# Lanes without a token gather a row of their own, and layer 1's row gathers wait for the landing three groups back

## The chip, the cores and the metric

The kernel runs on one core of a Trainium2 chip. The metric is the device time of one execution in microseconds (us), the median of several runs. Engines are named as the profile names them: PE (TensorE matmul), PEld (its weight load), DVE (VectorE), ACT (ScalarE), POOL (GpSimd) and SP (SyncE, which only issues DMAs here).

## The reference, cut to what matters

Two transformer layers over 4 x 1024 tokens of 128 features. Each layer ends in a feed-forward block with experts, in which one expert is chosen for each token. Layer 0 has 8 experts, layer 1 has 16 and a shared expert beside them:

```python
# layer 0: xt is (4096, 128)
probs = softmax(xt @ Wr + br);  gate, idx = max(probs), argmax(probs)
y = relu(xt @ W1[idx] + b1[idx]) @ W2[idx] + b2[idx]       # for each token its own expert
x = x + gb * y * gate
# layer 1
score = sigmoid(max(hidden @ router_w.T));  e = argmax
gate, up = split((hidden * score) @ gate_up_proj[e])
routed = (up * silu(gate)) @ down_proj[e]
shared = (silu(hidden @ shared_gate_w.T) * (hidden @ shared_up_w.T)) @ shared_down_w.T
x = x + gb * (shared + routed)
```

## The kernel before

**Tiles of one expert each.** The tokens of each expert are put into tiles of 128 lanes, and every expert starts a new tile. The number of tiles that this takes depends on the data, so the program always runs the most that can occur: `NS0 = NT + E0 = 40` in layer 0 and `NS1 = NT + E1 = 48` in layer 1 (`NT = 32` is 4096 tokens by 128). 48 tiles have 6144 lanes for 4096 tokens, so 2048 lanes of layer 1 hold no token (1024 in layer 0). Counting the experts that the router chooses for the reference's own inputs, the tokens of layer 1 fill or begin 39 tiles; tiles 39 to 47 hold no token at all. In layer 0 they take 37, and tiles 37 to 39 are empty.

**How the rows get into the tiles.** The normalised tokens lie in `M.h` (32 tiles of 128 x 128 f32) and are stored to HBM as `hrows0`, a row of 512 B for each token (SP, lines 255 to 258 in layer 0 and 1955 to 1961 in layer 1). The class `Dispatch` works out `gidx[lane, tile]`, the number of the row that a lane reads. In `sources` (lines 865 to 872) `psI[:, NS:2*NS]` is the token's tile plus 1, or 0 in a lane without token, and `psI[:, 0:NS]` is its lane. 128 x (tile plus 1) - 128, cut off at 0, plus the lane is the row. For a lane without token it gives 0: all of these lanes read row 0, the first token's. POOL then issues one indirect DMA (a gather of 128 rows, 64 KB) for each tile, line 984 in layer 0 and line 1997 in layer 1. The results of empty lanes are never read.

**The order around the change.** Each engine runs its own list in order, and engines wait for each other by semaphores. Tiles go in groups of `GT = 4`. In layer 1, POOL issues the 48 gathers; each adds to the semaphore `got` of its group (a ring of 4). Ahead of tile 8 POOL waits until groups 0 and 1 have landed, and ahead of each group q from 3 on until PE has turned group q - 2 (`x_T`). PE waits for `got` ahead of each group, turns the four tiles (line 2242), and then runs for each tile the two matmuls of line 2252, a transpose (line 2259) and the matmuls of line 2269. Gathers of tiles 0 to 31 land in `M.h`, those of tiles 32 to 47 in `spare`, a part of the buffer `shared_kept`, that the shared expert used before. Its last reader there is DVE (`gate`, which counts in `m_ready`).

**After the experts.** DVE copies each result to `y` (line 2149), SP stores it to `result1` (line 1965), and when all is stored POOL gathers the results back in token order (line 2007, 32 gathers). DVE multiplies and adds them (lines 2157 and 2164), between its steps for the last five parts of the shared expert (lines 1850, 1851, 1878, 1892 and 1903), and SP stores `out`.

Of the kernel before, what the change touches and what calls it, by code (L numbers as in the profile page):

```python
# [171 lines left out]
def phase_front(nc, D, M):  # L172

    at = turn_order()
    with Names(nc, "fr_") as n:
# [59 lines left out]
        with nc.Block() as block:  # L235
            @block.sync
            def _(sp):
                def load_x(b):
                    sp.dma_start(M.x[:, tiles_of(b), :], D["x"][b].rearrange("(t p) e -> p t e", p=P)).then_inc(ld_x[b], 16)

                sp.dma_start(cT[:], D["cT"]).then_inc(ld_c, 16)
                sp.dma_start(wmod0[:], D["wmod"][:, 0, :]).then_inc(ld_c, 16)
                load_x(0)
                for dst, src in qkv:
                    sp.dma_start(dst[:], src).then_inc(ld_qkv, 16)
                load_x(1)
                for dst, src in outer:
                    sp.dma_start(dst[:], src).then_inc(ld_o, 16)
                load_x(2)
                load_x(3)  # L250
                for dst, src in later[:EARLY_LOADS]:
                    sp.dma_start(dst[:], src).then_inc(ld_o, 16)
                for dst, src in later[EARLY_LOADS:]:
                    sp.dma_start(dst[:], src).then_inc(ld_later, 16)
                for b in range(B):
                    sp.wait_ge(h_ready, b + 1)
                    sp.dma_start(M.hrows0[b * L:(b + 1) * L, :].rearrange("(t p) e -> p t e", p=P),
                                 M.h[:, tiles_of(b), :]).then_inc(M.h_stored, 16)
                sp.wait_ge(ld_later, 16 * (len(later) - EARLY_LOADS))

# [480 lines left out]
class Dispatch:  # L741
# [123 lines left out]
    def sources(self, dve, link):  # L865

        NS = self.NS
        dve.wait_ge(self.inv_mm, 1)
        link(dve.tensor_scalar(self.tile_row[:], self.psI[:, NS:2 * NS], float(P), -float(P), ALU.mult, ALU.add))
        link(dve.scalar_tensor_tensor(out=self.tile_row[:], in0=self.tile_row[:], scalar=0.0, in1=self.psI[:, 0:NS],  # L870
                                      op0=ALU.max, op1=ALU.add))
        dve.tensor_copy(self.M.gidx[:, 0:NS], self.tile_row[:]).then_inc(self.idx_ready, 1)  # L872

    def ranks(self, pe):

# [32 lines left out]
def phase_ffn0(nc, D, M):  # L908

    E, NS = E0, NS0  # L910
    with Names(nc, "f0_") as n:
# [28 lines left out]
        with nc.Block() as block:  # L940
# [28 lines left out]
            @block.gpsimd  # L969
            def _(pool):  # L970
                link = Link(pool, pool_step)
                pool.wait_ge(M.h_stored, 16 * B)
                pool.wait_ge(disp.idx_ready, 1)

                for k in range(NS):
                    q = k // GT
                    if k % GT == 0:
                        if q >= 2 and q % 2 == 0:
                            pool.wait_ge(got[q - 1], 16 * GT)
                        if q == WINDOW:  # L980
                            pool.wait_ge(x0_T, GT)
                        elif q > WINDOW:
                            pool.wait_ge(x_T, q - WINDOW)
                    pool.indirect_dma_start(  # L984
                        out=row_tile(k), out_offset=None, in_=M.hrows0[:, :],
                        in_offset=bass.IndirectOffsetOnAxis(ap=M.gidx[:, k:k + 1], axis=0)).then_inc(first[k] if q == 0 else got[q], 16)
                bounded_gate_on(pool, link, M, tmp, 0, GB)
                pool.wait_ge(mod_out, B)
                cb = M.mod[:, 1, :, CB * P:(CB + 1) * P]
                link(pool.tensor_scalar(cb, cb, 1.0, None, ALU.add))  # L990
                bounded_gate_on(pool, link, M, tmp, 1, GA)
                bounded_gate_on(pool, link, M, tmp, 1, GB)
                for s in first:
                    pool.wait_ge(s, 16)
                for s in got[1:]:
                    pool.wait_ge(s, 16 * GT)
# [912 lines left out]
def phase_ffn1(nc, D, M):  # L1909

    E, NS, NC = E1, NS1, 2 * B
    with Names(nc, "f1_") as n:
# [3 lines left out]
        h_ready, h_T, hT_ready, lg_mm = n.sem("h_ready"), n.sem("h_T"), n.sem("hT_ready"), n.sem("lg_mm")  # L1916
        shifted, exp_done, gate_ready, rows_ready = n.sem("shifted"), n.sem("exp_done"), n.sem("gate_ready"), n.sem("rows_ready")
        ld_shared, ld_experts, h_stored = n.sem("ld_shared"), n.sem("ld_experts"), n.sem("h_stored")
        got = [n.sem(f"got{i}") for i in range(WINDOW + 1)]
        x_T, xT_ready, mm1_done, silu_done, g_ready = (n.sem("x_T"), n.sem("xT_ready"), n.sem("mm1_done"),  # L1920
                                                       n.sem("e_silu_done"), n.sem("g_ready"))
        g_T, gT_ready, mm2_done, y_ready = n.sem("g_T"), n.sem("gT_ready"), n.sem("mm2_done"), n.sem("y_ready")
# [25 lines left out]
        with nc.Block() as block:  # L1948
            @block.sync
            def _(sp):  # L1950
                for dst, name in ((M.wsg1, "wsg1"), (M.wsd1, "wsd1")):
                    sp.dma_start(dst[:], D[name]).then_inc(ld_shared, 16)
                for dst, name in ((M.wgu1, "wgu1"), (M.wdn1, "wdn1")):
                    sp.dma_start(dst[:], D[name]).then_inc(ld_experts, 16)
                for b in (B - 1, *range(B - 1)):
                    if b == B - 1:
                        sp.wait_ge(last_rows, 1)
                    else:
                        sp.wait_ge(rows_ready, b + 1)
                    sp.dma_start(hrows[b * L:(b + 1) * L, :].rearrange("(t p) e -> p t e", p=P),  # L1960
                                 M.h[:, b * TB:(b + 1) * TB, :]).then_inc(h_stored, 16)
                rows_out = M.result1.rearrange("(s p) e -> p s e", p=P)
                for q in range(NS // GT):
                    sp.wait_ge(y_ready, (q + 1) * GT)
                    sp.dma_start(rows_out[:, q * GT:(q + 1) * GT, :], y[q % 2]).then_inc(stored[q % 2], 16)
                for c in range(NC):
                    sp.wait_ge(x_steps, c + 1)
                    sp.wait_ge(shared.x_added, c + 1)
                    sp.dma_start(D["out"][c // 2].rearrange("(t p) e -> p t e", p=P)[:, 4 * (c % 2):4 * (c % 2) + 4, :],
                                 M.x[:, 4 * c:4 * c + 4, :]).then_inc(out_stored, 16)  # L1970
                sp.wait_ge(out_stored, 16 * NC)

            @block.gpsimd
            def _(pool):
# [14 lines left out]
                pool.wait_ge(disp.idx_ready, 1)  # L1989
                for k in range(NS):  # L1990
                    q = k // GT
                    if k == 2 * GT:
                        for done in range(2):
                            pool.wait_ge(got[done], 16 * GT)
                    if k % GT == 0 and q >= WINDOW:
                        pool.wait_ge(x_T, q - WINDOW + 1)
                    pool.indirect_dma_start(  # L1997
                        out=row_tile(k), out_offset=None, in_=hrows[:, :],
                        in_offset=bass.IndirectOffsetOnAxis(ap=M.gidx[:, k:k + 1], axis=0)).then_inc(got[q % len(got)], 16)
# [313 lines left out]
def declare(nc, M):  # L2313
# [9 lines left out]
    M.gate, M.zeros = M.sb("gate", [P, NT]), M.sb("zeros", [P, P])  # L2323
    M.slot, M.expert = M.sb("slot", [P, NT], I32), M.sb("expert", [1, NS1], I32)
    M.result1 = nc.dram_tensor("result1", [NS1 * P, P], F32).ap()
    M.hrows0 = nc.dram_tensor("hrows0", [NT * P, P], F32).ap()
    M.result0 = nc.dram_tensor("result0", [NS0 * P, P], F32).ap()
    M.gidx = M.sb("gidx", [P, NS1], I32)
    M.lane, M.pcol, M.ip1 = M.sb("lane", [P, P]), M.sb("pcol", [P, 1]), M.sb("ip1", [P, NT])
# [95 lines left out]
```

## Time and profile before

| | us |
|---|---|
| median of 3 runs | 1177.31 |
| lowest and highest run | 1174.46 and 1179.62 |
| the profiled execution | 1174.11 |
| its span in the trace | 1172.1 |
| outside the span (1174.11 - 1172.1) | 2.0 |

The profiled execution lies 3.2 us under the median of the three runs. Times in the rows are us from the span's start. In the span the layers' stages follow one another: layer 0's attention until about 130, layer 0's experts from 130 to 223, layer 1's attention until about 985, and layer 1's feed-forward block from there to the end.

### The profile page before, as it was taken

To read this page: it belongs to the slowest core of one execution; us is meant where nothing else is said; L and a number is where in the kernel's file an instruction comes from. 1 tells how busy PE (TensorE), PEld (TensorE's weight loads), DVE (VectorE), ACT (ScalarE), POOL (GpSimd) and SP (SyncE) were. 2 spreads that over 40 slices of the span, in tenths; PEclk is the share of its full clock that TensorE was granted. 3 is DMA by queue.
4 is the path that set the end of the run, shared out by engine and by line. 5 is a ranking of instruction groups with operands and counts; after the bars stand their busy time and mean duration, and the time that the engine had idled before them with its cause. 6 is when DMAs were issued, how large, how long until landed. Compare 5 with 4: busy or idle time off the path is not lost. (4 is left out here: it accounts for less than half of the span.)

```text
span 1172.1 us, 23749 instructions
## 1 busy us (share of the span) xinstructions
PE 1045.9 (89%) x9028; PEld 496.0 (42%) x9028; DVE 946.6 (81%) x1442; ACT 780.5 (67%) x1559; POOL 332.0 (28%) x467
## 2 busy tenths in 40 slices
PE   6897699587679999999999999999999989889797
PEld 4786599443311222222222222222222249467555
DVE  7975555478799999999999999999999719956345
ACT  4543334144414999999999999999999976524221
POOL 4732367667520000000000000000000026257264
PEclk9988899898976999999999999999999999999899
DMA  7011377319980012220122201222020002314623
GB/s 239 1 37 37 86 202 203 106 34 215 215 200 2 22 16 34 35 34 15 23 34 36 34 5 33 35 35 34 4 34 3 3 2 81 111 53 116 66 61 84
DMA packets 93975, 76.75 MB, mean 65 GB/s; under 512 B 42884, under 2 KB 72836, under 8 KB 93352
## 3 DMA queue, kind: packets, MB, share of 16 engines
q1 hardware_dynamic: 89000, 65.27, 23.6%
q0 software_dynamic: 4864, 9.97, 4.9%
q8 instruction: 73, 1.20, 0.5%
q14 instruction: 38, 0.31, 0.1%
HBM read 47.74 MB, written 27.39 MB: 64 GB/s over the span
## 5 line engine op out<-in xcount | busy, mean ns | idle before, releaser
L1462 DVE TENSOR_REDUCE mx<-p_psA 128x1 f32<-128x1024 f32 x512 | 585.1, 1214 | 9.4 <-PE p_psA L1625 9.4
L1553 ACT ACTIVATE p_pt<-p_psS 128x512 f32<-128x512 f32 x1024 | 548.2, 596 | 37.8 <-PE p_psS L1647 18.1
L1660 PE MATMUL p_acc<-p_pt,V 128*32 128x256 f32 x4096 | 328.4, 392 | 15.4 <-ACT attn L1544 13.8
L1625 PE MATMUL p_psA<-K,Q 48*128 48x512 bf16 x1024 | 319.8, 395 | 9.4 <-DVE mx L1462 7.8
L1647 PE MATMUL p_psS<-Q,K 51*128 51x512 bf16 x1024 | 310.0, 384 | 0.0
L1660 PEld LDWEIGHTS p_acc<-p_pt,V 128*32 128x32 f32 x4096 | 81.9, 108 | 211.1 <-ACT p_pt L1553 110.5
L1379 POOL TENSOR_TENSOR mr<-zeros,mx 128x16 f32<-128x16 f32 x32 | 7.1, 223 | 546.8 <-DVE mx L1462 546.8
L1625 PEld LDWEIGHTS p_psA<-K,Q 48*128 48x128 bf16 x1024 | 57.0, 95 | 232.8 <-DVE mx L1462 197.8
L1647 PEld LDWEIGHTS p_psS<-Q,K 51*128 51x128 bf16 x1024 | 62.6, 93 | 18.1 <-ACT p_pt L1553 12.6
L1067 DVE TENSOR_TENSOR f_h<-f_bank,b 128x512 f32<-128x512 f32 x40 | 27.7, 692 | 38.3 <-PE f_bank L1135 38.3
L1027 ACT ACTIVATE f_h1T<-f_h 128x512 f32<-128x512 f32 x40 | 25.1, 629 | 31.2 <-DVE f_h L1067 31.2
L2061 ACT ACTIVATE f_sg<-f_bank 128x128 f32<-128x128 f32 x48 | 13.3, 278 | 48.2 <-PE f_bank L2252 48.2
L1135 PE MATMUL f_bank<-f_xT,f_w 128*128 128x128 f32 x320 | 43.6, 281 | 0.0
L1144 PE MATMUL f_mod_ps<-w,f_h1T 128*128 x320 | 42.7, 279 | 0.0
L2007 POOL DMA_INDIRECT h<-result,slot x32 | 31.0, 968 | 36.7 <-DMA result<-f_shared_kept 18.9
L984 POOL DMA_INDIRECT h<-hrows,gidx x32 | 30.6, 955 | 38.2 <-DVE gidx L872 20.9
L1135 PEld LDWEIGHTS f_bank<-f_xT,f_w 128*128 128x128 f32 x320 | 40.3, 197 | 0.1
L1997 POOL DMA_INDIRECT h<-hrows,gidx x32 | 31.6, 988 | 29.6 <-DVE gidx L872 18.0
L1144 PEld LDWEIGHTS f_mod_ps<-w,f_h1T 128*128 128x128 f32 x320 | 39.6, 195 | 0.0
L1334 POOL DMA_INDIRECT h<-result,slot x32 | 33.2, 1036 | 18.7 <-issue 7.8
L1850 PE MATMUL f_bank<-hT_l,wsg 128*128 128x512 f32 x64 | 34.5, 621 | 3.6 <-ACT f_shared_kept L1861 1.9
L1865 ACT ACTIVATE f_shared_sg<-f_bank 128x512 f32<-128x512 f32 x20 | 11.9, 597 | 36.6 <-PE f_bank L1850 36.6
(336 smaller groups left out, 1442.1 us busy)
## 6 DMA issues: line engine op xcount, KB each, us to landing
f_w<-in_w SPq DMA_DIRECT2D x40, 256.0 KB, 3.6
Q<-q_rows SPq DMA_DIRECT2D x32, 192.0 KB, 4.6
K<-k_rows SPq DMA_DIRECT2D x32, 192.0 KB, 5.2
hrows<-h SPq DMA_DIRECT2D x8, 512.0 KB, 3.2
result<-f_shared_kept SPq DMA_DIRECT2D x12, 256.0 KB, 3.0
result<-f_y SPq DMA_DIRECT2D x10, 256.0 KB, 4.1
V<-v_rows SPq DMA_DIRECT2D x16, 144.0 KB, 5.8
x<-in_x SPq DMA_DIRECT2D x4, 512.0 KB, 5.5
```

The costliest lines, as they stand in the source:

```text
L984: pool.indirect_dma_start(out=row_tile(k), out_offset=None, in_=M.hrows0[:, :], in_offset=bass.IndirectOffsetOnAxis(ap=M.gidx[:, k:k + 1], ...
L1135: mm = pe.matmul(ps1[j % 2][:, c * P:(c + 1) * P], w1[j % RING][:, c * P:(c + 1) * P], xT[j // GT % 2][:, j % GT, :], start=True, stop=True)
L1144: mm = pe.matmul(psY[j % 2][:, 0:P], h1T[j % RING][:, c, :], M.w20[:, bass.ds(expert[j], 1), c, :], start=(c == 0), stop=(c == FC0 - 1))
L1334: pool.indirect_dma_start(out=M.h[:, i, :], out_offset=None, in_=M.result0[:, :], in_offset=bass.IndirectOffsetOnAxis(ap=M.slot[:, i:i + 1 ...
L1462: dve.tensor_reduce(mx[v % 2][:, h, qt:qt + 1], psA[t][:], AX.X, ALU.max).then_inc(a_max, 1)
L1553: act.activation(pt[s % 2][:, head_at(s, j), :], psS[k % 3][:], ACT.Exp, scale=INV_SCALE).then_inc(s_out, 1)
L1625: mm = pe.matmul(psA[t][:, c * 512:(c + 1) * 512], Q[g % NBUF][rows, pair, q0:q0 + P], K[g % NBUF][rows, pair, c * 512:(c + 1) * 512], sta ...
L1647: pe.matmul(psS[k % 3][:], K[g % NBUF][rows, h // 2, kc * P:(kc + 1) * P], Q[g % NBUF][rows, h // 2, half * 512:(half + 1) * 512], start=T ...
L1660: mm = pe.matmul(acc[VW * h:VW * (h + 1), cols], V[g % NBUF][:, kc, h * (HD + 1):h * (HD + 1) + VW], pt[s % 2][:, h, cols], start=(kc == 0 ...
L1850: pe.matmul(self.bank_g(k)[:], M.wsg1[:, f * P:(f + 1) * P], tok, start=True, stop=True).then_inc(self.g_mm, 1)
L1997: pool.indirect_dma_start(out=row_tile(k), out_offset=None, in_=hrows[:, :], in_offset=bass.IndirectOffsetOnAxis(ap=M.gidx[:, k:k + 1], ax ...
L2007: pool.indirect_dma_start(out=M.h[:, i, :], out_offset=None, in_=M.result1[:, :], in_offset=bass.IndirectOffsetOnAxis(ap=M.slot[:, i:i + 1 ...
```

## The change

Four edits. (1) `hrows0` gets 128 rows more, in front of the token rows; SP fills them once, at the start, with the identity matrix `M.ident` (64 KB), and stores the tokens 128 rows further on, in both layers. (2) `sources` no longer takes off 128, and its last step is a maximum with `pcol` (a column that holds the lane's number) in place of a copy: a token's row number is now at least 128 and stays, and a lane p without token gets row p. (3) POOL's gathers of layer 1 have a semaphore for each group of four, and ahead of group q from 3 on POOL waits until group q - 3 has landed, not for PE; the wait ahead of tile 8 goes. (4) Since nothing then ties POOL to PE, it waits for `m_ready` ahead of tile 32, the first in `shared_kept`.

```diff
@@ SP, start of the program
+                sp.wait_ge(ld_qkv, 16 * len(qkv))
+                sp.dma_start(M.hrows0[0:P, :], M.ident[:]).then_inc(M.h_stored, 16)
                 for b in range(B):
                     sp.wait_ge(h_ready, b + 1)
-                    sp.dma_start(M.hrows0[b * L:(b + 1) * L, :].rearrange("(t p) e -> p t e", p=P),
+                    sp.dma_start(M.hrows0[P + b * L:P + (b + 1) * L, :].rearrange("(t p) e -> p t e", p=P),
                                  M.h[:, tiles_of(b), :]).then_inc(M.h_stored, 16)
@@ Dispatch.sources (DVE, both layers)
-        link(dve.tensor_scalar(self.tile_row[:], self.psI[:, NS:2 * NS], float(P), -float(P), ALU.mult, ALU.add))
+        link(dve.tensor_scalar(self.tile_row[:], self.psI[:, NS:2 * NS], float(P), None, ALU.mult))
         link(dve.scalar_tensor_tensor(out=self.tile_row[:], in0=self.tile_row[:], scalar=0.0, in1=self.psI[:, 0:NS],
                                       op0=ALU.max, op1=ALU.add))
-        dve.tensor_copy(self.M.gidx[:, 0:NS], self.tile_row[:]).then_inc(self.idx_ready, 1)
+        dve.tensor_scalar(self.M.gidx[:, 0:NS], self.tile_row[:], self.M.pcol[:, 0:1], None, ALU.max).then_inc(self.idx_ready, 1)
@@ layer 0, POOL
-                pool.wait_ge(M.h_stored, 16 * B)
+                pool.wait_ge(M.h_stored, 16 * (B + 1))
@@ layer 1
-        got = [n.sem(f"got{i}") for i in range(WINDOW + 1)]
+        got = [n.sem(f"got{i}") for i in range(NS // GT)]
@@ layer 1, SP
-                    sp.dma_start(hrows[b * L:(b + 1) * L, :].rearrange("(t p) e -> p t e", p=P),
+                    sp.dma_start(hrows[P + b * L:P + (b + 1) * L, :].rearrange("(t p) e -> p t e", p=P),
@@ layer 1, POOL
-                    if k == 2 * GT:
-                        for done in range(2):
-                            pool.wait_ge(got[done], 16 * GT)
+                    if k == NT:
+                        pool.wait_ge(shared.m_ready, EK)
                     if k % GT == 0 and q >= WINDOW:
-                        pool.wait_ge(x_T, q - WINDOW + 1)
+                        pool.wait_ge(got[q - WINDOW], 16 * GT)
@@ declare
-    M.hrows0 = nc.dram_tensor("hrows0", [NT * P, P], F32).ap()
+    M.hrows0 = nc.dram_tensor("hrows0", [P + NT * P, P], F32).ap()
```

What stands in a row on POOL in layer 1's gathers, before. A semaphore's number serves several phases and is named here after the first of them, so only the places of the waits tell something: the two names ahead of tile 8 are the landings of groups 0 and 1, the single name from tile 12 on is PE's `x_T`.

```order
L1997 DMA h<-hrows,gidx 128x128 [waits f1_idx_ready,fr_mod_ready]
L1997 DMA h<-hrows,gidx 128x128 x7
L1997 DMA h<-hrows,gidx 128x128 [waits fr_rstd_ready,fr_stats_ready]
L1997 DMA h<-hrows,gidx 128x128 x3
L1997 DMA h<-hrows,gidx 128x128 [waits fr_norm2_act]
L1997 DMA h<-hrows,gidx 128x128 x3
```

The same place of the changed kernel, and below "..." its first gather into `shared_kept`:

```order
L1998 DMA h<-hrows,gidx 128x128 [waits f1_idx_ready,fr_mod_ready]
L1998 DMA h<-hrows,gidx 128x128 x11
L1998 DMA h<-hrows,gidx 128x128 [waits fr_stats_ready]
L1998 DMA h<-hrows,gidx 128x128 x3
L1998 DMA h<-hrows,gidx 128x128 [waits fr_rstd_ready]
L1998 DMA h<-hrows,gidx 128x128 x3
...
L1998 DMA f_shared_kept<-hrows,gidx 128x128 [waits fr_act_step,f1_m_ready]
L1998 DMA f_shared_kept<-hrows,gidx 128x128 x3
```

The first twelve gathers now stand in a row without a wait; from tile 12 on a wait for a landing (another semaphore each time) stands where the wait for PE stood, and tile 32 has `m_ready` as well.

On SP, between the loads at the start of the program and the stores of the token rows, there was before:

```order
L254 DMA bo<-in_bo 128x128
L254 DMA wr<-in_wr 128x16
L257 DMA hrows<-h 128x8x128 [waits fr_h_ready] x4
L235 UNCONDITIONAL_BRANCH [waits fr_ld_later]
```

and now:

```order
L254 DMA bo<-in_bo 128x128
L254 DMA wr<-in_wr 128x16
L256 DMA hrows<-ident 128x128 [waits fr_ld_qkv]
L259 DMA hrows<-h 128x8x128 [waits fr_h_ready] x4
L235 UNCONDITIONAL_BRANCH [waits fr_ld_later]
```

One DMA more, behind all loads and ahead of the first store of rows.

## Rows read from the trace of the kernel before

**Rows 1.** The page: the span and the packets of the queue that POOL's gathers use.
```profile
span 1172.1 us, 23749 instructions
...
q0 software_dynamic: 4864, 9.97, 4.9%
```

**Rows 2.** The chain that ended last, in order of time: start, us, what.
```profile
1027.89 0.52 PE f_bank L895 x8
...
1072.55 0.64 PE f_bank L2242 x4
...
1092.28 9.75 DMA f_shared_kept<-hrows,gidx
1102.08 0.66 PE f_bank L2242 x4
...
1109.12 2.28 DMA result<-f_shared_kept
...
1112.14 0.94 POOL h L2007
...
1115.89 3.10 DMA h<-result,slot
1119.02 0.70 DVE f_shared_kept L2157
```

**Rows 3.** Timeline of PE, layer 1's experts: start, us, instruction [idle before <-releaser].
```profile
1047.61 0.60 PE L2242 MATMUL f_bank<-ident,h 128*128 128x128 f32 x4
...
1076.65 0.63 PE L2242 MATMUL f_bank<-ident,h 128*128 128x128 f32 x4
...
1080.74 0.63 PE L2242 MATMUL f_bank<-ident,f_shared_kept 128*128 128x128 f32 x4
...
1087.17 0.66 PE L2242 MATMUL f_bank<-ident,f_shared_kept 128*128 128x128 f32 x4 [2.35 <-DMA f_shared_kept<-hrows,gidx]
...
1095.30 1.11 PE L2242 MATMUL f_bank<-ident,f_shared_kept 128*128 128x128 f32 x4 [4.04 <-DMA f_shared_kept<-hrows,gidx]
```

**Rows 4.** Timeline of POOL, layer 1's gathers.
```profile
1042.68 1.43 POOL L1997 DMA_INDIRECT h<-hrows,gidx  x1 [2.24 <-DMA h<-hrows,gidx]
...
1048.48 0.95 POOL L1997 DMA_INDIRECT h<-hrows,gidx  x1 [0.60 <-PE f_bank L2242]
...
1077.24 0.95 POOL L1997 DMA_INDIRECT f_shared_kept<-hrows,gidx  x1 [0.30 <-issue]
...
1091.03 0.95 POOL L1997 DMA_INDIRECT f_shared_kept<-hrows,gidx  x1 [0.30 <-issue]
1092.28 0.94 POOL L1997 DMA_INDIRECT f_shared_kept<-hrows,gidx  x1 [0.30 <-issue]
```

**Rows 5.** DMA queues from 1060 to 1074: packets, MB, share of 16 engines.
```profile
q0 software_dynamic: 361, 0.75, 23.9%
q1 hardware_dynamic: 1584, 0.79, 19.5%
```

**Rows 6.** The same from 1085 to 1099.
```profile
q0 software_dynamic: 225, 0.46, 85.2%
q1 hardware_dynamic: 528, 0.26, 6.2%
```

**Rows 7.** Stretches: length, busy us of PE, PEld, DVE, ACT, POOL, PEclk, DMA share, GB/s.
```profile
1094.00:1100.00 6.00, 4.70 (x16) 3.89 (x17) 1.86 (x5) 0.98 (x4) 0.00 (x0) 0.50 0.85 54
...
1121.00:1160.00 39.00, 38.91 (x182) 24.47 (x183) 18.07 (x28) 8.36 (x14) 23.37 (x25) 1.00 0.25 68
```

**Rows 8.** Line 1997: its gathers' time from issue to landing.
```profile
DMA to landing us min/median/max: 2.5/2.9/3.6
```

**Rows 9.** Layer 0, timelines of POOL (L984) and PE (L1121).
```profile
130.42 1.22 POOL L984 DMA_INDIRECT h<-hrows,gidx  x1 [20.93 <-DVE gidx L872]
...
181.46 0.94 POOL L984 DMA_INDIRECT f_spare<-hrows,gidx  x1 [3.24 <-DMA h<-hrows,gidx]
...
190.21 0.95 POOL L984 DMA_INDIRECT f_spare<-hrows,gidx  x1 [0.30 <-issue]
...
142.97 1.12 PE L1121 MATMUL f_bank<-ident,h 128*128 128x128 f32 x4 [4.19 <-DMA h<-hrows,gidx]
...
206.12 0.60 PE L1121 MATMUL f_bank<-ident,f_spare 128*128 128x128 f32 x4
```

**Rows 10.** Timelines of SP at the start, and of DVE in layer 1's routing.
```profile
22.55 0.76 SPq L254 DMA_DIRECT2D wr<-in_wr  x1
65.64 44.23 SPq L257 DMA_DIRECT2D hrows<-h  x4
...
1028.44 0.21 DVE L869 TENSOR_SCALAR f_tile_row<-f_bank 128x48 f32<-128x48 f32 x1 [0.61 <-PE f_bank L895]
...
1028.92 0.19 DVE L872 CAST gidx<-f_tile_row 128x48 int32<-128x48 f32 x1
```

## The prediction, made before the changed kernel ran

> **What bounds the kernel now.** I read the chain that ended last first, because the change touches only two short stretches of a long kernel. In layer 1's experts the chain runs over PE up to 1072.55, then over POOL's issues to the last one at 1092.28, then through 9.75 us of a gather in flight, to PE's last group at 1102.08 [rows 2]. So the end of the expert stage is set by the landing of the last gather, and all behind it is tied to it: the store of the last results (1109.12), the gathers back (1112.14), and DVE's first use of them (1119.02), which stands ahead of DVE's steps for the shared expert [rows 2].
>
> Next, the timeline of PE. Groups 7 and 8 are turned at 1076.65 and 1080.74: 4.10 us for a group when nothing is missing [rows 3]. (Groups 2 to 8 all keep this step.) Group 9 then starts at 1087.17 after 2.35 us of idling, group 10 at 1095.30 after 4.04 us, both released by gathers [rows 3], group 11 at 1102.08 [rows 2]. With PE alone they would stand at 1084.84, 1088.94 and 1093.04.
>
> Why do these gathers land so late? POOL issues one each 1.25 us (1091.03 to 1092.28) [rows 4], and one normally lands 2.5 to 3.6 us after its issue, median 2.9 [rows 8]. The DMA queues show it. The program has 152 gathers (40 and 48 of rows in, 32 and 32 back) and 4864 packets on their queue [rows 1], 32 for each. From 1060 to 1074, 361 packets took 23.9% of 16 engines' 14 us [rows 5]: 53.5 us, 0.148 us each, so 32 of them keep the 16 engines for 0.30 us. From 1085 to 1099, 225 packets took 85.2% [rows 6]: 190.8 us, 0.85 us each, 1.70 us for a gather. That is more than the 1.25 us between two issues, so a backlog grows.
>
> What differs in these gathers? Not other traffic: the other queue took 19.5% in the quick stretch and 6.2% in the slow one [rows 5, 6]. Not the destination: group 8 goes to the same buffer, its last gather was issued at 1077.24 [rows 4] and PE started on it at 1080.74 without idling [rows 3], so it landed within 3.5 us. What differs is the content: tiles 39 to 47 hold no token, and each of their 128 lanes reads row 0. The late groups are just those with these tiles (9, 10 and 11). I conclude that 128 reads of one row of HBM are served nearly one after the other.
>
> **The change part by part.** The rows of empty lanes (edits 1 and 2). In the changed kernel a gather of an empty tile reads 128 different rows, 64 KB in a piece. No such gather is in the trace. Bounds: as quick as a gather of token rows, 0.30 us of the engines [rows 5], or no quicker than now, 1.70 us [rows 6]. I take the first, since there too all rows differ. The choice need not be exact: anything under POOL's 1.25 us leaves no backlog.
>
> POOL's waits (edit 3). Two stalls go: 2.24 us ahead of tile 8 and 0.60 us ahead of tile 12 [rows 4], each less the 0.30 us that stands ahead of every issue: 1.94 + 0.30 = 2.24 us. The new wait holds all later gathers and the gathers back behind it. It is for a gather issued 9 places back, 9 x 1.25 = 11.3 us, against a landing after 3.6 us at the most [rows 8]; even 9.75 us [rows 2] is under it. It costs nothing. The wait for `m_ready` ahead of tile 32 costs nothing either: PE's experts start, behind the shared parts that it counts, at 1047.61 [rows 3], some 24 us before tile 32 is issued. POOL's last issue moves from 1092.28 to 1090.04.
>
> Which is then the last? By POOL: 1090.04 and the time from a gather's issue to its reader. In the quiet stretch behind, that was 1119.02 - 1115.89 = 3.13 us [rows 2]. This gives group 11 at 1093.17. By PE: 1093.04. The two are almost level, and the later one gives 1102.08 - 1093.17 = **8.9 us saved**. With a landing of 3.6 us in place of 3.1 it would be 8.4, and never more than PE's 9.04 us. Groups 9 and 10 come out the same way: their last gathers are issued at about 1080.0 and 1085.0 and are there at 1083.2 and 1088.2, before PE wants them at 1084.84 and 1088.94. PE's clock, 0.50 from 1094 to 1100 [rows 7] behind its idling, counts for nothing in the sum, since PE waited for landings before and after that stretch.
>
> The Trainium skill (DMA: Bandwidth & Descriptors, the section on the anatomy of one DMA) gives the time of such a DMA as about 2.0 us plus bytes by 436 GB/s, whatever it reads; for 64 KB that is an estimate of 2.15 us, for the nine empty tiles as for any. This trace doesn't agree: 0.30 and 1.70 us of the engines for the same bytes. By the page, lane addresses would not matter and edits 1 and 2 would bring nothing; that is the first rival below.
>
> Does the gain reach the end? Between 1102.08 and 1119.02 each link waits for the one before [rows 2], and then PE is busy 38.91 of the 39 us from 1121 to 1160 [rows 7] with work that DVE's first use of the results released. Nothing there has a start of its own, so the whole moves forward.
>
> What it costs. DVE's last step of the routing: the copy took 0.19 us and a `TENSOR_SCALAR` of the same size 0.21 [rows 10]: 0.02 us, twice, and dropping the addition saves nothing that shows: 0.0. The identity rows: one more issue on SP (0.76 us for the one before it) into the idle time between 23.3 and 65.64 [rows 10]; its landing is asked for only ahead of the first gather at 130.42 [rows 9]. It costs nothing while that gap is there, and 0.8 us if it weren't. PE's first links of the stage (L895 at 1027.89 [rows 2]) don't change.
>
> Layer 0. It has the same cure for tiles 37 to 39, but no path to shorten. Their last gather is issued at 190.21 and PE turns that group at 206.12 [rows 9], 15.9 us later, with no idling between. POOL's stalls there (3.24 us ahead of tile 32, others alike) stay and are hidden too. PE's idle 4.19 us ahead of 142.97 [rows 9] is for group 1, in which the counts put only nine empty lanes: between 0 and 0.4 us, and I take 0.
>
> The sum: 1174.11 - 8.9 = 1165.2 us for the profiled execution. The median of the runs shown lies 3.2 us over that execution, so I forecast a median of 1177.31 - 8.9 = **1168.4 us**, 0.76% less. A measurement of this kernel can tell about 0.5%, 5.9 us, from no change.
>
> **The rivals.** (a) The row isn't the cause, and gathers of empty tiles stay at 1.70 us. Then only the 2.24 us of POOL's stalls remain, since the backlog begins that much earlier: 1175.1, no change that can be told. For it: no row of before has an empty tile that reads different rows. Against it: destination and traffic are excluded above, and only these nine tiles are slow. 10%.
>
> (b) The clock. It falls to half for stretches like the 6 us from 1094 on [rows 7]. If such a stretch comes into the shared part, in which PE bounds and now has 1.00 from 1121 to 1160 [rows 7], it costs up to 6.0 x 0.5 = 3.0 us: 1171.4. Against it: the fall at 1094 stood behind PE's idling of 2.35 and 4.04 us, and just this idling goes. 6%.
>
> (c) Slower: different rows are read worse than one row, for all nine tiles come back to the same 64 KB shortly after each other. The nine gathers begin to be read near 1083 and now end at 1102. (1102.1 - 1083.1) / 9 = 2.1 us for a gather is the point from which the kernel is slower; at 3.4 us, twice the present 1.70, the last lands near 1083.1 + 30.6 = 1113.7, 11.6 us late: 1188.9. For it speaks only that it isn't in the trace; against it the quick gathers of token rows. 4%.
>
> **How the numbers follow.** The forecast has 80%: 1168.4. Its own range goes from the lowest of the three runs less PE's 9.04 us, 1165.4, to the highest less 8.4, 1171.2. I take 1.1 us more below, since three runs may not show their lowest and layer 0 may give 0.4, and reach up to 1172.5, which takes in (b) with an unlucky median; (a) and (c), 14%, are left out. Faster by over 0.5%: the forecast and half of (b), 0.83. Within: (a) and the other half of (b), 0.13. Slower: 0.04.
>
> **What would show it.** In the trace of after: PE without idling ahead of groups 9 to 11, group 11 near 1093; POOL's last issue of a row gather near 1090; less than 35% of the engines for POOL's queue in the last 14 us of the gathers, and about 0.30 us a gather; no fall of the clock there; the back gathers starting near 1103; layer 0 as long as before. The cause is wrong if tiles 39 to 47 still take over 1.25 us each; the path is wrong if group 11 starts near 1093 and the end has not moved by 8 to 9 us.

## The result, and the profile after

| | before | after |
|---|---|---|
| median of 4 runs, us | 1176.26 | 1163.84 |
| lowest and highest | 1174.46 and 1179.62 | 1162.37 and 1166.31 |
| profiled execution | 1174.11 | 1166.31 |
| its span | 1172.1 | 1164.2 |

The ratio of the times is 0.9895, with a 95% interval from 0.9871 to 0.9918: 9.6 to 15.2 us saved, 12.4 between the medians. The forecast was 8.9 us saved and a range down to 1164.3, and the median lies 0.5 us below that range. The two profiled executions differ by 7.9 us. The difference between 7.9 and 12.4 is where these two executions lie among the runs: before 2.2 us under its median, after 2.5 us over it, as the slowest of four. That the kernel would later be slower than before on other chips could not be seen here; it is told below.

The traces show the forecast's path. PE's timeline in layer 1 (start, us, instruction), the last step of the routing and then groups 0, 8 and 11 of the kernel after:

```profile
1027.22 0.52 PE L897 MATMUL f_bank<-f_who,f_ohlo 128*128 128x96 bf16 x8 [0.78 <-DVE f_ohlo L855]
...
1048.64 0.60 PE L2243 MATMUL f_bank<-ident,h 128*128 128x128 f32 x4
...
1081.76 0.63 PE L2243 MATMUL f_bank<-ident,f_shared_kept 128*128 128x128 f32 x4
...
1094.06 0.63 PE L2243 MATMUL f_bank<-ident,f_shared_kept 128*128 128x128 f32 x4
```

The rows with idle times of [rows 3] are gone: from group 8 to 11 there are three steps of 4.10 us, 12.30 in all, where before they took 21.34 (1080.74 to 1102.08): 9.04 us less. POOL's timeline, the first and the last row gather and the first gather back:

```profile
1029.28 1.39 POOL L1998 DMA_INDIRECT h<-hrows,gidx  x1 [18.01 <-DVE gidx L874]
...
1089.22 0.94 POOL L1998 DMA_INDIRECT f_shared_kept<-hrows,gidx  x1 [0.30 <-issue]
1104.09 0.94 POOL L2008 DMA_INDIRECT h<-result,slot  x1 [13.92 <-DMA result<-f_shared_kept]
```

The last row gather is issued at 1089.22 (forecast 1090.04, with a stage that begins 0.6 us earlier), and the gathers back begin at 1104.09 in place of 1112.14 [rows 2]. The queues over the last 14 us of the row gathers, 1077 to 1091 (packets, MB, share of 16 engines), and line 1998's landings:

```profile
q0 software_dynamic: 362, 0.76, 21.0%
q1 hardware_dynamic: 1586, 0.79, 19.5%
```
```profile
DMA to landing us min/median/max: 2.4/2.5/3.5
```

21.0% of 16 x 14 us for 362 packets is 0.13 us a packet, 0.26 us of the engines for a gather, where the gathers of empty tiles had 1.70 [rows 6]. They are as cheap as gathers of tokens.

One thing had moved the other way. These are stretches of the kernel after (length, busy us of PE, PEld, DVE, ACT and POOL, PEclk, DMA share, GB/s), the first in the shared part ahead of the experts:

```profile
1028.00:1031.00 3.00, 3.00 (x5) 1.17 (x4) 2.95 (x7) 0.60 (x1) 1.41 (x2) 0.50 0.00 0
1094.00:1100.00 6.00, 5.69 (x36) 4.58 (x35) 3.92 (x14) 2.87 (x14) 0.00 (x0) 1.00 0.21 64
```

and this is the first of them in the kernel before:

```profile
1028.00:1031.00 3.00, 3.00 (x15) 1.56 (x15) 2.49 (x7) 1.19 (x2) 1.11 (x1) 1.00 0.00 0
```

The clock is 1.00 from 1094 to 1100, where it was 0.50 before [rows 7]. But it had fallen to half, 1.2 GHz, at 1028, in a part in which PE sets the pace. PE had idled three times in the routing just ahead of it, for 0.7 to 0.8 us each; before, it idled there in the same way, and the clock stayed at 1.00. So these two traces don't show why it fell. Group 0 is turned 21.4 us after PE's last step of the routing (line 897, 1027.22), where before it was 19.7 us (1027.89 to 1047.61). This execution lost 1.7 us there, and without it would have saved 9.6. In terms of the last group: 9.04 us gained by PE, 1.7 lost to the clock and 0.7 by which the routing ended earlier give 8.0, and group 11 stands 8.02 us earlier.

### The profile page after: what moved, and what is told of

The parts are those of the page before. It is cut to its first block and busy times, and to the rows that moved or that the text cites. A ratio compares the mean times of both kernels' runs of the same rounds, so it can differ in the third digit from the quotient of the medians.

```text
span 1164.2 us, 23750 instructions
## 1 busy us (share of the span) xinstructions
PE 1044.9 (90%) x9028; PEld 493.3 (42%) x9028; DVE 948.4 (81%) x1442; ACT 780.3 (67%) x1559; POOL 329.8 (28%) x467
## 5 line engine op out<-in xcount | busy, mean ns | idle before, releaser
L1029 ACT ACTIVATE f_h1T<-f_h 128x512 f32<-128x512 f32 x40 | 25.2, 629 | 31.5 <-DVE f_h L1069 31.5
L986 POOL DMA_INDIRECT h<-hrows,gidx x32 | 30.5, 953 | 38.0 <-DVE gidx L874 20.9
```

Of the source, the lines that this page charges most:

```text
L986: pool.indirect_dma_start(out=row_tile(k), out_offset=None, in_=M.hrows0[:, :], in_offset=bass.IndirectOffsetOnAxis(ap=M.gidx[:, k:k + 1], ...
```

## The experiments

I made 18 runs on five chips. The first eight fell on chips 14 and 8, the next four on chip 9, four on chip 6 and the last two on chip 10. It turned out that there are two kinds of chips here, so the kernel before stands beside each. The chip of the first measurement has no number on record.

### The parts alone, on chips 14 and 8

Own rows without the new waits, against the change (also rows_only_2 and rows_only_3):

```diff
-                    if k == NT:
-                        pool.wait_ge(shared.m_ready, EK)
+                    if k == 2 * GT:
+                        for done in range(2):
+                            pool.wait_ge(got[done], 16 * GT)
                     if k % GT == 0 and q >= WINDOW:
-                        pool.wait_ge(got[q - WINDOW], 16 * GT)
+                        pool.wait_ge(x_T, q - WINDOW + 1)
```

> Each empty lane reads a row of its own, in both layers, but the row gathers of layer 1 keep the waits of the kernel before (groups 0 and 1 landed ahead of tile 8, PE's transposes from tile 12 on). Row theory: tiles 39 to 47 land as quickly as any; the last issue stays near 1092.3, the last group starts at 1092.3 + 3.1 = 1095.4 in place of 1102.1, so 6.7 us are saved and PE waits about 1 to 2 us in all for rows. Rival (the row is not the cause): tiles 39 to 47 stay at 1.70 us of the engines each, and nothing is saved. If another 3 us of the measured gain (12.4 us between the medians, where the two profiled spans differ by 7.9) also belong to the rows, this kernel saves 9 to 10 us.

The new waits without own rows, against the kernel before (also waits_only_2 and waits_only_3):

```diff
-        got = [n.sem(f"got{i}") for i in range(WINDOW + 1)]
+        got = [n.sem(f"got{i}") for i in range(NS // GT)]
@@ layer 1, POOL
-                    if k == 2 * GT:
-                        for done in range(2):
-                            pool.wait_ge(got[done], 16 * GT)
+                    if k == NT:
+                        pool.wait_ge(shared.m_ready, EK)
                     if k % GT == 0 and q >= WINDOW:
-                        pool.wait_ge(x_T, q - WINDOW + 1)
+                        pool.wait_ge(got[q - WINDOW], 16 * GT)
```

> Empty lanes read row 0 as before; the row gathers of layer 1 wait for the landing three groups back. Row theory: the gathers of empty tiles still take 1.70 us each and only start 2.24 us earlier, so 2.2 us are saved and PE still waits some 5 to 7 us ahead of groups 9 to 11. Rival: the waits bring the greater part, 6 us or more. If the new wait can hold POOL, it shows here, where landings are latest: an idle time of POOL ahead of one of the last groups.

Own rows in layer 1 only, against the change:

```diff
-        dve.tensor_scalar(self.M.gidx[:, 0:NS], self.tile_row[:], self.M.pcol[:, 0:1], None, ALU.max).then_inc(self.idx_ready, 1)
+        if NS == NS1:
+            dve.tensor_scalar(self.M.gidx[:, 0:NS], self.tile_row[:], self.M.pcol[:, 0:1], None, ALU.max).then_inc(self.idx_ready, 1)
+        else:
+            dve.tensor_copy(self.M.gidx[:, 0:NS], self.tile_row[:]).then_inc(self.idx_ready, 1)
```

> The changed kernel, but in layer 0 the empty lanes read row 0 (all the same row, as before); layer 1 as changed. Theory that layer 0 hides its three empty tiles behind 15.9 us of slack: the time of the changed kernel within 0.5 us, about 1164. Rival, that the surplus of the measured gain over 8.9 us comes from layer 0: 3 us slower than the changed kernel, about 1167.

And the changed kernel itself:

> The changed kernel once more, beside the others on one chip. If the gain is the 9 us of PE's path, five rounds give 1167 beside 1176; if the measured gain of 12 us is real they give 1164. The trace shows which of the two profiled spans was the odd one: with no fall of the clock in the shared part ahead of the experts, group 0 starts about 1.0 to 1.7 us earlier than 1048.64 and the span is near 1162.

Measured on chip 14 (median us; ratio to the kernel before, 1203.06):

| kernel | us | ratio, 95% interval |
|---|---|---|
| rows_only | 1203.25 | 0.9995 (0.9971 to 1.0019) |
| waits_only | 1237.12 | 1.0283 (1.0246 to 1.0321) |
| rows_layer1 | 1239.61 | 1.0298 (1.0259 to 1.0337) |
| after_again | 1238.71 | 1.0306 (1.0268 to 1.0344) |

None of my numbers held except that layer 0's rows make no difference (rows_layer1 against after_again, within 1 us of each other). The kernel before was 27 us slower than on the first chip, and the changed kernel was slower than it by 36 us. The new waits alone made it so. (That layer 0's rows make no difference is thus measured on this chip alone.) I asked four again, with the kernel before for its trace:

> The kernel before, unchanged, for its trace. In the last four runs the kernel before took 1203 us and the changed kernel 1239, where the first measurement gave 1176 and 1164; there PE stood still for up to 2.4 us between two matmuls while POOL issued gathers. If that belongs to the chip, one of two pictures comes: 1176 and PE without such gaps ahead of 1080, or 1203 with gaps of 1 to 4 us in PE from tile 12 of the gathers on. In either, the last group is turned 9.0 us or more behind PE's own pace (tiles 39 to 47 read one row).

> The changed kernel once more. If the odd times belong to the chip of the last runs and this is another: 1164 to 1168, 9 to 12 us under the kernel before. If they come from the changed kernel itself (POOL issuing all 48 gathers without a pause), it is slower than the kernel before again, by 30 us or more, wherever it runs.

> Own rows for empty lanes, with the waits of before, once more. Where PE has no gaps: 6.7 us under the kernel before by my sum (the last gather issued near 1092.3, its group started at 1095.4), and 9 to 10 us if the surplus over the forecast belongs to the rows. Where PE has gaps: no difference, as in the last runs, since PE and not the last landing ends the stage.

> Row 0 for all empty lanes, with the new waits, once more. Where PE has no gaps: 2.2 us under the kernel before, PE waiting 5 to 7 us for the last three groups. Where PE has gaps: 30 us slower than before, since POOL then isn't paced by PE.

They came to chip 8 and repeated the picture beside the kernel before at 1203.88 (19 runs): before_again 1203.29, after_third 1236.15 (1.027, 1.0214 to 1.0325), rows_only_2 1204.18 (0.9995, 0.997 to 1.002) and waits_only_2 1236.2 (1.0244, 1.0203 to 1.0284).

Where does the time go? PE's timeline of after_again, in the shared part of layer 1 ahead of the experts (line 1894, 96 small matmuls; 10.7 us in the kernel before):

```profile
1052.28 6.86 PE L1894 MATMUL f_bank<-wsd,f_m 128*128 128x128 f32 x58
1060.69 0.60 PE L1894 MATMUL f_bank<-wsd,f_m 128*128 128x128 f32 x4 [1.54 <-issue]
...
1098.68 0.37 PE L1894 MATMUL f_bank<-wsd,f_m 128*128 128x128 f32 x1 [2.43 <-issue]
1101.48 0.37 PE L1894 MATMUL f_bank<-wsd,f_m 128*128 128x128 f32 x1 [2.43 <-issue]
...
1109.88 0.37 PE L1894 MATMUL f_bank<-wsd,f_m 128*128 128x128 f32 x1 [2.43 <-issue]
1111.28 0.37 PE L1894 MATMUL f_bank<-wsd,f_m 128*128 128x128 f32 x1 [1.03 <-issue]
...
1113.38 1.23 PE L1894 MATMUL f_bank<-wsd,f_m 128*128 128x128 f32 x5 [0.33 <-issue]
```

From 1082 on PE issues one matmul each 2.8 us and waits for nothing that the profile knows; ahead of that its gaps are shorter, mostly 1.0 to 1.8 us. POOL's timeline of the same run shows when this begins and ends:

```profile
1045.34 1.39 POOL L1998 DMA_INDIRECT h<-hrows,gidx  x1 [18.02 <-DVE gidx L874]
...
1059.94 0.95 POOL L1998 DMA_INDIRECT h<-hrows,gidx  x1 [0.30 <-issue]
...
1105.41 0.94 POOL L1998 DMA_INDIRECT f_shared_kept<-hrows,gidx  x1 [0.30 <-issue]
```

The first gap opens at 1059.14 (1052.28 + 6.86), between the issues of the eleventh and the twelfth gather in an unbroken row, and the last one of 2.43 us ends at 1109.88, 4.5 us behind the last issue. In the kernel before the waits break this row up: POOL stops ahead of tile 8 and then for PE. On chip 8 the kernel before has such gaps as well, but fewer and shorter ones. This is POOL in before_again, and below it PE's last group there:

```profile
1109.27 0.95 POOL L1997 DMA_INDIRECT f_shared_kept<-hrows,gidx  x1 [1.34 <-remote]
...
1115.35 0.94 POOL L1997 DMA_INDIRECT f_shared_kept<-hrows,gidx  x1 [1.39 <-remote]
...
1121.42 0.95 POOL L1997 DMA_INDIRECT f_shared_kept<-hrows,gidx  x1 [1.36 <-remote]
```
```profile
1136.12 0.63 PE L2242 MATMUL f_bank<-ident,f_shared_kept 128*128 128x128 f32 x4
```

A group takes 6.07 us there where PE alone needs 4.10. PE idles about 2 us in each group and POOL 1.3 us between two groups, for PE's turning of an earlier one: as I read it, they hold each other back. The last landing ends nothing (PE turns group 11 without idling), and own rows have nothing to shorten (rows_only 0.9995 twice). That the row cost itself is the same on these chips is told by the queue of waits_only on chip 14, from 1101 to 1110, and of after_again, from 1098 to 1107:

```profile
q0 software_dynamic: 166, 0.35, 88.8%
```
```profile
q0 software_dynamic: 224, 0.46, 19.1%
```

0.77 us a packet with row 0 for all, 0.12 with own rows.

### What keeps PE from issuing

Four kernels that change only the row gathers of layer 1. plain_pool and plain_sp replace them by plain loads, half_rows halves their bytes, paced spreads them by a multiplication on POOL ahead of each but the first (its operand is cleared once at the start):

```diff
@@ plain_pool (plain_sp: the same loop on SP)
-                    pool.indirect_dma_start(
-                        out=row_tile(k), out_offset=None, in_=hrows[:, :],
-                        in_offset=bass.IndirectOffsetOnAxis(ap=M.gidx[:, k:k + 1], axis=0)).then_inc(got[q % len(got)], 16)
+                    r = P + (k % NT) * P
+                    pool.dma_start(row_tile(k), hrows[r:r + P, :]).then_inc(got[q % len(got)], 16)
@@ half_rows
-                        out=row_tile(k), out_offset=None, in_=hrows[:, :],
+                        out=row_tile(k)[:, 0:P // 2], out_offset=None, in_=hrows.rearrange("r (a e) -> (r a) e", a=2),
@@ paced (filler, filler2: 128 x 256; declared and cleared above)
+                    if k > 0:
+                        link(pool.tensor_tensor(filler2[:], filler[:], filler[:], ALU.mult))
```

> POOL's 48 row gathers of layer 1 are replaced by plain DMAs that POOL issues: tile k loads 128 rows that follow one another, whichever tokens they are, so the routed results are not the reference's; waits, bytes and destinations as in the changed kernel. Question: what keeps PE from issuing (up to 2.4 us between two matmuls) on the chips where the changed kernel takes 1236 to 1239 us. Theory A, POOL's way of issuing (it writes the descriptors of each DMA): the gaps stay, about 1236. Theory B, the indirection itself: the gaps go, about 1180. If the kernel before takes 1176 here, there are no gaps to explain and the time is near 1160.

> The same plain loads, issued by SP with the same waits; POOL issues nothing until the gathers back. Again the routed results are not the reference's. Theory A (POOL's issuing disturbs PE): PE has no gaps in layer 1's experts, groups of 4.1 us, about 1180 where the changed kernel takes 1236. Theory C (the transfers themselves, 64 KB in 128 descriptors of 512 B, whoever issues them): gaps as in the changed kernel, 1236.

> The row gathers of layer 1 bring only the first 256 B of a row's place (a wrong half row for most lanes, so the routed results are not the reference's), with as many descriptors. If bytes are what matters, PE's gaps shrink by about half and 1236 becomes 1200 to 1210; if the number of gathers or descriptors matters, nothing changes: 1236.

> The changed kernel with a small multiplication on POOL (128 x 256, some 0.6 us) and its semaphore between two row gathers of layer 1, so that they come each 2 us and not each 1.25. If gathers issued too closely fill something that PE needs (the sum of issues and pauses in the runs so far fits with one gather each 2 us as what it can bear), PE's gaps go and its part of the shared expert ahead of the experts ends near 1064 in place of 1114; the last gather is then issued near 1045 + 47 x 2 = 1139 and the kernel takes about 1215 in place of 1236. If each gather costs PE a fixed time, however they are spaced, it stays at 1236 or is slower.

They came to chip 9, where the kernel before takes 1180.16 and PE has no gaps: 1166.73, 1169.58, 1168.89 and 1196.5 us, one execution each. On the gaps they say nothing. They do say what ends the stage. With plain loads all rows are there long before they are needed, and from the first load to PE's last group it is still 64.5 us (plain_pool, 1030.29 to 1094.82), as from the first gather in the changed kernel, 64.8 (1029.28 to 1094.06): PE alone bounds the stage by now. And paced shows the chain: PE waits for landings again, its last group starts at 1123.39 and not at 1094.06 (29.3 us later), and the span is 1194.7 and not 1164.2 (30.5 us longer).

The last two runs repeated two of them, and came to chip 10 (kernel before 1206.21, one execution):

> Plain loads of 128 consecutive rows in place of layer 1's row gathers, issued by POOL at 0.54 us each (the routed results are not the reference's). Only a chip of the kind of 14 and 8 (kernel before near 1203) tells something: about 1236 if any DMA that POOL issues keeps PE from issuing, about 1190 if it takes indirect gathers. On a chip of the other kind (kernel before near 1177): 1166, as twice.

> The changed kernel with a small POOL instruction between the row gathers of layer 1, so that they come each 1.9 us. On a chip of the kind of 14 and 8: if what counts is how closely gathers are issued, PE's gaps shrink or go, its shared part ends before 1075, and the kernel takes about 1215, less than the changed one (1236); if each gather costs PE a fixed time, 1236 or more. On a chip of the other kind: 1196, as once.

plain_pool_3 took 1188.84, paced_2 1215.81. Two rows of PE's timeline in plain_pool_3, the first of the experts and the next row with an idle time behind 1074 (46 us later), and then the list of PE's waits in paced_2 from 1040 to 1160 (us, times, longest), its first three:

```profile
1071.96 1.12 PE L2252 MATMUL f_bank<-wgu,f_shared_kept 128*128 x4 [1.76 <-DVE f_shared_kept L2137]
...
1120.17 0.48 PE L2269 MATMUL f_bank<-wdn,f_gT 128*128 x2 [0.17 <-ACT f_gT L2067]
```
```profile
PE f_bank L2247 <- DMA h<-hrows,gidx: 11.1, 5, 3.5
PE f_bank L2247 <- DMA f_shared_kept<-hrows,gidx: 10.0, 4, 3.7
PE f_bank L897 <- DVE f_ohlo L855: 2.3, 3, 0.8
```

Both expectations held on this chip, the first within 2 us. Without indirect gathers in layer 1 PE has no gap there, although POOL issues its DMAs faster (0.54 us each). With indirect gathers 1.9 us apart it has none either: no wait for "issue" is left in the list, where after_again had 42.4 us of them.

This tells something only if chip 10 has gaps at all, and neither of its runs is the changed kernel. Layer 0 settles it. Its 40 row gathers are indirect in every kernel of this document and 1.25 us apart, up to eight in a row. In plain_pool_3, POOL's first of them, and then PE:

```profile
130.58 1.21 POOL L986 DMA_INDIRECT h<-hrows,gidx  x1 [20.64 <-DVE gidx L874]
```
```profile
136.89 0.33 PE L1115 MATMUL f_bank<-ident,h 128*128 128x128 f32 x1 [0.85 <-issue]
...
164.81 1.15 PE L1146 MATMUL f_mod_ps<-w,f_h1T 128*128 x8 [1.59 <-issue]
...
220.78 0.60 PE L1123 MATMUL f_bank<-ident,f_spare 128*128 128x128 f32 x4
```

From the first gather to PE's last group layer 0 takes 90.2 us here, and 75.7 in the kernel before [rows 9]. The same stretch sorts all traces: 86.7 to 91.0 us in the ten from chips 14, 8 and 10, whatever the kernel, and 74.6 to 76.6 in the other ten. So one execution on chip 10 has gaps where gathers are 1.25 us apart and none where plain loads are 0.54 us apart, and another (paced_2) none where gathers are 1.9 us apart. On these three chips it is indirect gathers issued close together that keep PE from issuing. In layer 0 they do so within the first eight gathers, so the number after which it begins is not fixed. It also explains the kernel before on these chips: in before_again layer 0's stretch is 12.7 us longer than in the first trace of before (88.4 against 75.7) and layer 1's, from the first gather to group 11, 12.5 us (84.7 against 72.2). That is 25.2 us, where the medians on chips 8 and 6 lie 26 us apart. (The execution before_again is itself a long one of its kernel, and its span exceeds the first by 35.7 us; the rest lies elsewhere.)

The paced kernel on chip 10 is 20 to 23 us faster than the changed one on chips 14 and 8 (a comparison across chips), but still slower than the kernel before by 10 us, since 48 gathers then take 91 us. What gathers and PE share is not settled. In after_again no fetch of instructions is recorded from 1056 to 1112, where the changed kernel had six packets of them on the first chip: more fetching is not the cause, but a fetch that is held back is not excluded.

### The parts alone, where PE has no gaps

> The changed kernel. Where the kernel before takes 1176 to 1180: 9 to 12 us less, PE without idling ahead of its last groups; 9 if the surplus of the first measurement was chance, 12 if it is real. Where the kernel before takes 1203: 33 to 36 us more, as twice now.

> Own rows, waits of before. Without gaps in PE: 6.7 us saved (last gather issued near 1092.3, last group at 1095.4), so about 2.2 us behind the changed kernel. With gaps: as the kernel before, as twice now.

> Row 0 for all empty lanes, new waits. Without gaps in PE: 2.2 us saved, PE still waiting 5 to 7 us for its last groups; the queue of POOL's gathers takes over 80% of the 16 engines in the last 14 us. With gaps: 33 us slower than before.

> Plain loads of 128 consecutive rows in place of layer 1's row gathers, issued by POOL (the routed results are not the reference's). On chip 9 it took 1166.7, PE without gaps. On a chip with gaps: about 1236 if any DMA that POOL issues makes them, about 1190 if only indirect gathers do.

All four ran on chip 6, with the kernel before at 1177.3 (19 runs):

| kernel | us | ratio, 95% interval | saved, us | first gather to last group, us |
|---|---|---|---|---|
| after_fourth | 1169.37 | 0.9936 (0.9913 to 0.996) | 7.9 | 1033.07 to 1097.86: 64.8 |
| rows_only_3 | 1172.7 | 0.9966 (0.995 to 0.9983) | 4.6 | 1031.25 to 1096.16: 64.9 |
| waits_only_3 | 1176.76 | 0.9995 (0.9978 to 1.0013) | 0.5 | 1034.84 to 1104.73: 69.9 |
| plain_pool_2 | 1166.33 | 0.9914 (0.9888 to 0.9939) | 11.0 | |

In the profiled execution of the kernel before the last column is 72.2 us (1029.89 to 1102.08). By it rows_only_3 saves 7.3 (expected 6.7), waits_only_3 saves 2.3 (expected 2.2) and after_fourth 7.4. By the medians the first expectation missed: 6.7 us lies outside what rows_only_3 saved (2.0 to 5.9), and after_fourth stayed under the 9 to 12 us that I expected, though 9 is within its interval (4.7 to 10.2). PE in waits_only_3, groups 10 and 11, and the queues from 1089 to 1103:

```profile
1097.57 0.66 PE L2241 MATMUL f_bank<-ident,f_shared_kept 128*128 128x128 f32 x4 [2.00 <-DMA f_shared_kept<-hrows,gidx]
...
1104.73 0.66 PE L2241 MATMUL f_bank<-ident,f_shared_kept 128*128 128x128 f32 x4 [1.78 <-DMA f_shared_kept<-hrows,gidx]
```
```profile
q0 software_dynamic: 229, 0.48, 89.7%
q1 hardware_dynamic: 1056, 0.52, 12.5%
```

229 packets took 200.9 us of engines (89.7% of 16 x 14 us), 0.88 each. The new waits have changed nothing in that; the same packets are quick as soon as each lane reads its own row. And rows_only_3, its last group:

```profile
1096.16 0.66 PE L2244 MATMUL f_bank<-ident,f_shared_kept 128*128 128x128 f32 x4 [1.04 <-DMA f_shared_kept<-hrows,gidx]
```

Here the landing still ends the stage, by 1.04 us, because POOL keeps its two stalls.

after_fourth, waits_only_3 and plain_pool_2 had the same 21.4 us from the last step of the routing to group 0 as the first profile of the changed kernel, with its fall of the clock; rows_only_3 and the kernel before did not (19.7 us). Each of these is one execution, and rows_only and rows_only_2 on the other chips had 21.4 us too, so I don't claim that the change brings the fall about. But it explains how the changed kernel and rows_only_3 come to the same 64.8 and 64.9 us: without these 1.7 us after_fourth would have needed 63.1, and what the waits gave it, the clock had taken.

## Why the prediction was right or wrong

**The cause held.** 128 reads of one row are slow, and the same reads of 128 rows are not: 0.77 to 0.88 us a packet against 0.12 to 0.13, shown with nothing else changed (waits_only against after_again). How the memory serves such reads is not shown: that it takes them "nearly one after the other" was my reading of the times. Of my two bounds for an empty tile, the quick one was right (0.26 us against 0.30). By the Trainium skill (DMA: Bandwidth & Descriptors, the anatomy of one DMA) both would take the same time, as their bytes are the same. The traces don't agree: the last one-row gather landed 9.75 us after its issue, with others queued ahead of it [rows 2], and every gather of the changed kernel within 2.4 to 3.5 us. Rival (a) is out, and so is (c).

**The path held.** Groups 9 to 11 follow without idling, PE is the last in the stage, and the rest moves with it: from group 11 to the end of the span there are 70.0 us before (1172.1 - 1102.08) and 70.1 after (1164.2 - 1094.06). Layer 0 gave nothing: from its first gather to its last group it took 75.7 us before and 75.6 after, and rows_layer1 agrees.

**The sum held, the range did not.** The term of the stage was 8.9 us, and the traces show 9.04 for it. The two measurements on chips without gaps gave 12.4 us saved (9.6 to 15.2) and 7.9 (4.7 to 10.2), on either side of it. The first, by which the forecast is judged, lies outside: the median came out 0.5 us under the range.

The step that failed is the one that turned the sum into a median and a range. It put the median of the runs 3.2 us over the profiled execution. The profiled execution was forecast at 1165.2 and took 1166.31, but the median of the four runs lay 2.5 us under it. For the spread I took three runs of the kernel before and allowed 1.1 us beyond them, down to 1164.3; two of the four runs were under that (1162.37 and 1162.65), and the fourth run of the kernel before moved its own median from 1177.31 to 1176.26. The kernel before then ran from 1172.96 to 1181.07 on chip 6, 8 us; of such runs the median of four is off by 2 us or more in one case of ten. The fall of the clock in the shared part, 1.7 us, is one piece of that spread, and rival (b) had its size: 3.0 us forecast at the most, for a stretch of 6 us, where one of some 3 us came, in another part of the shared expert.

What stays open is the gain itself on the first chip. Its interval begins at 9.6 us, over the 9.04 that I had called the most that PE can give, and no trace shows where more would come from. Chip 6, with 7.9, speaks for chance in a few runs; it doesn't prove it.

**One step was wrong, and the first chip hid it.** "It costs nothing", on the new wait. As a wait it never held POOL, on any chip. But the old wait had done something that I hadn't asked about: it kept POOL's gathers from running in an unbroken row. Without it the changed kernel was 32 to 36 us slower than the kernel before on chips 14 and 8 (on chip 10 it wasn't run). I looked for what is queued behind the added wait and not for what the removed wait had held apart. No row of before shows it, since on its chip nothing happens; my rivals had no case of it.

What would one keep? On chip 6 the changed kernel is ahead (7.9 us against 4.6, with intervals that overlap); on 14 and 8 rows_only equals the kernel before and the changed kernel loses 32 to 36. Own rows with the old waits was never slower in these runs.

## What to carry to other kernels

Lanes without work should not all read one address: give each its own row, and look at the busy share of the DMA queue against the bytes moved to find such a place. When a wait is removed, ask what rate it had imposed, and not only who waited for it. And a gain of under 1% should be measured on more than one chip.

## What the runs showed of the hardware that I had not expected

A gather of 128 rows from one address took the 16 engines 1.5 to 1.8 us, where one from 128 addresses took 0.24 to 0.30 (traces of the first chip and of chips 14 and 6). On chips 14, 8 and 10, indirect gathers issued by POOL 1.25 us apart kept PE from issuing, with waits that the profile puts down to nothing: in layer 0 within the first eight gathers, and in the unbroken row of layer 1 (chips 14 and 8) down to one matmul in 2.8 us. Plain loads issued 0.54 us apart did not, nor did gathers 1.9 us apart (both on chip 10, one execution each). On chips 9 and 6 no such gap came with the same gathers. The kernel before takes 1203 to 1206 us on the first three chips against 1177 to 1180 on the other two, and its two stretches of row gathers are longer there by 25 us together (chip 8, one execution).
